# Attention scores as pairs of 64-row products, and softmax sums that are packed, inverted and spread by DMA

## Chip, cores and metric

One core of a Trainium2 chip runs the whole kernel in one launch. The metric is the device time of a run in microseconds; lower is better. The names of the engines are TensorE (PE, with its weight loads PEld), VectorE (DVE), ScalarE (ACT), GpSimd (POOL) and SyncE (SP), which only issues DMA transfers here.

## What is computed

The reference is two transformer-like layers on x of shape (2, 512, 512), all in float32: modulation, layer norm, attention, a routed low-rank expert block, then a second layer with weights in a 4-bit code. The change touches the attention of the first layer only:

```python
# 32 heads of size 16; 8 groups of keys and values, 4 heads to a group; S = 512
q = (x @ wq).reshape(b, s, 32, 16)
k = (x @ wk).reshape(b, s, 8, 16)      # each repeated for its 4 heads
v = (x @ wv).reshape(b, s, 8, 16)
scores = einsum('bihd,bjhd->bhij', q, k) * 16 ** -0.5
scores = where(causal, scores, finfo.min)
attn = softmax(scores, axis=-1)
out = einsum('bhij,bjhd->bihd', attn, v).reshape(b, s, 512)
return out @ wo
```

## The kernel before

Every engine has its program written out by hand; they meet at semaphores. The program runs through: modulation and layer norm with the projections of q, k and v (to 88 us of the trace), the attention stage (about 89 to 297 us), the output projection, the expert block, and the second layer, which takes two thirds of the time. While attention runs, the first 4-bit weights are decoded beside it in steps (`step_at`): ScalarE makes curves (L777), VectorE sums them (L1095), GpSimd scales them.

**Precision by parts.** A float32 value is kept as a rounded high part and a low part (FH and FL for the queries, KH and KL for the keys), and products are made of the parts.

**Stacks.** One stack holds one batch b and one group g: its number is n = 8 b + g, 16 in all, in three buffers. In `QS` (queries, stationary) rows 0 to 63 hold high, high, low, low parts of the group's 16 rows for 4 heads; in `KS` and `KN` (keys, moving) they hold high, low, high, low. The product over these 64 rows gives the exact score. Rows 64 to 127 of KS are zero; those of QS take a diagonal of the row maxima (L678, GpSimd), those of KN are -1. `load_stack` (L497, on SP) fills a stack by 12 transfers from SBUF to SBUF, four of 128 KB and eight of 32 KB. It waits until the stack three back is used up (`s_st`).

**Units.** A stack has four units, one for each block of 128 queries; unit n of 64 has (n % 4 + 1) * 128 keys, by causality. TensorE's order at step n is:
- `scores(n)` (L1532): for each of two halves, when the maxima of the same half of unit n - 1 are there, two heads of score products over 128 rows (L1540), each followed by a mask product of identB and maskB over 128 columns (L1542), then a signal. Four PSUM banks, one a head.
- `transposed(n - 2)` (L1546): the score products again with keys as output rows, now with KN, so that the maximum is subtracted (L1555, one per block of keys, three PSUM banks in turn, and a mask at L1558).
- on even n, `weighted(n - 4)` and `weighted(n - 3)` (L1563): exponentials times values, in four column tiles of 32, one a head (L1572, float32). V holds ones beside the values, so the sums of the softmax come out too, into bank 7.

VectorE at unit n takes the maxima of two heads twice (L1229), then the curve sum if one is due (slots 0, 1 and 7 of each eight units), then the work on a pair of groups: `copy_odd` in slot 2 (L1153, L1155) adds the odd group's bank 7 to NUM (values) and DEN (sums), of which ScalarE has copied the even group's (`copy_even`, L519); `swap_sums` in slot 3 shuffles the sums below the values they belong to (L1161); `invert` in slots 4 and 5 is a reciprocal of 256 columns each (L1165); `divide` in slot 6 (L1170). ScalarE takes the exponentials (L817) and rounds the divided heads (L797); VectorE splits them (L1177). The last pair's steps come after the loop.

## Time and profile before

| | |
|---|---|
| runs | 974.74, 969.53, 973.49 us; median 973.49 |
| profiled execution | 974.34 us, its span 972.50 us |
| mean granted TensorE clock | 0.97 of full speed |
| busy over the span | TensorE 891.2 us (92%), VectorE 707.7 (73%), ScalarE 528.5 (54%), GpSimd 190.3 (20%) |
| attention stage | 89 to 297 us |
| row maxima L1229 | 128 instructions, 99.6 us on VectorE |
| score products L1540 | 256 instructions |
| packets of DMA over the span | 91.6 MB, mean 94 GB/s |

Times are of one profiled execution, from the start of its span. Matmuls are pipelined: start plus duration of one is where it ends, and durations of neighbours overlap, so work on TensorE is best counted from end to end. A row of the timeline may hold several instructions of one kind (x24). "idle before <-releaser" tells how long the engine stood before an instruction and who ended that.

### The profile page before, as it was taken

The numbers are of one execution on the slowest core, as the hardware profiler recorded it, in microseconds if no ns is written. First come the engines' busy times: TensorE is split into PE (matmuls) and PEld (weight loads), VectorE is DVE, ScalarE is ACT, GpSimd is POOL, SyncE is SP. The second block draws the span as 40 slices with busy tenths as digits, with TensorE's granted clock in tenths as the row PEclk, the third lists the DMA queues.
The fourth block names the chain that finished last, engine by engine and source line by source line (L and its number), as shares of the span: only waits on it lengthen the run. The fifth ranks groups of instructions, "written<-read, shape, count | busy, mean of one in ns | idle before, by whom it ended". The sixth has DMA issues, their size and how long they took to land.

```text
span 972.5 us, 13806 instructions
## 1 busy us (share of the span) xinstructions
PE 891.2 (92%) x5240; PEld 684.8 (70%) x5240; DVE 707.7 (73%) x907; ACT 528.5 (54%) x695; POOL 190.3 (20%) x197
## 2 busy tenths in 40 slices
PE   3698899989889789897999999999969999999996
PEld 2456555556557568686888888688857888888885
DVE  4735789888879778788887776367887666766842
ACT  1512656656663424476766666366727666666830
POOL 3002456477557112300000000000040000000004
PEclk9798999999999989999999999889989999999999
DMA  9387466566534003105334323023312333332202
GB/s 325 104 270 150 57 102 108 73 106 109 67 71 158 11 13 101 29 22 155 109 99 113 107 88 95 14 86 98 108 34 62 106 93 87 109 97 71 71 1 87
DMA packets 40162, 91.61 MB, mean 94 GB/s; under 512 B 6944, under 2 KB 10144, under 8 KB 40096
## 3 DMA queue, kind: packets, MB, share of 16 engines
q1 hardware_dynamic: 35824, 85.23, 34.7%
q10 hardware_dynamic: 4272, 5.49, 1.6%
q8 instruction: 42, 0.69, 0.3%
q14 instruction: 24, 0.20, 0.1%
HBM read 76.02 MB, written 2.10 MB: 80 GB/s over the span
## 4 chain that ended last, share of the span: by engine, by line
PE 68%; DVE 5%; issue 3%; POOL 1%; ACT 1%; POOLq 0%; DVEq 0%; ACTq 0%
PE PS L1438 14%; PE PS L1439 14%; PE PS L1440 14%; PE PS L1749 5%; PE PS L1750 5%; PE PS L1748 5%; PE PS L1540 2%; PE PS L1572 1%; PE PS L1731 1%; POOL X L662 1%; PE PS L1555 1%; DVE MX L1229 1%; PE PS L1478 1%; PE PS L1490 1%; DVE SCR L1080 1%
## 5 line engine op out<-in xcount | busy, mean ns | idle before, releaser
L777 ACT ACTIVATE PL<-CODE 128x1024 f32<-128x1024 int32 x200 | 201.6, 1056 | 40.9 <-DVE ACC L1095 38.3
L1438 PE MATMUL PS<-HH,WRH 128*128 128x512 f32 x448 | 175.3, 391 | 0.0
L1439 PE MATMUL PS<-HH,WRL 128*128 128x512 f32 x448 | 175.1, 391 | 0.0
L1440 PE MATMUL PS<-HL,WRH 128*128 128x512 f32 x448 | 174.9, 390 | 0.0
L662 POOL TENSOR_TENSOR X<-X,SCR 128x512 f32<-128x512 f32 x32 | 42.1, 1326 | 574.3 <-DVE SCR L1080 574.2
L1095 DVE SCALAR_TENSOR_TENSOR ACC<-PL,ACC 128x1024 f32<-128x1024 f32 x100 | 124.5, 1245 | 8.4
L817 ACT ACTIVATE PT<-PS 128x512 f32<-128x512 f32 x160 | 85.2, 604 | 68.3 <-PE PS L1555 49.2
L1229 DVE TENSOR_REDUCE MX<-PS 128x2 f32<-128x256 f32 (+3 forms) x128 | 99.6, 818 | 20.2 <-PE PS L1542 12.7
L678 POOL TENSOR_TENSOR QS<-ident,MX 64x256 fp32r<-64x256 f32 x128 | 97.0, 758 | 68.1 <-DVE MX L1229 61.1
L1540 PE MATMUL PS<-KS,QS 128*128 128x128 f32 (+3 forms) x256 | 84.3, 411 | 15.8 <-DVE MX L1229 14.3
L1438 PEld LDWEIGHTS PS<-HH,WRH 128*128 128x128 f32 x448 | 84.6, 189 | 18.1 <-issue 0.8
L1440 PEld LDWEIGHTS PS<-HL,WRH 128*128 128x128 f32 x448 | 84.4, 188 | 17.5
L1439 PEld LDWEIGHTS PS<-HH,WRL 128*128 128x128 f32 x448 | 84.5, 189 | 17.0
L1385 DVE TENSOR_TENSOR HID<-SG,PS 128x512 f32<-128x512 f32 x56 | 38.2, 684 | 76.8 <-PE PS L1440 74.5
L1748 PE MATMUL PS<-WRH,HH 128*128 128x512 f32 x216 | 85.0, 394 | 0.0
L1750 PE MATMUL PS<-WRH,HL 128*128 128x512 f32 x216 | 84.9, 393 | 0.0
L1749 PE MATMUL PS<-WRL,HH 128*128 128x512 f32 x216 | 84.9, 393 | 0.0
L1540 PEld LDWEIGHTS PS<-KS,QS 128*128 128x128 f32 x256 | 51.3, 202 | 28.9 <-issue 14.0
L1095 DVE SCALAR_TENSOR_TENSOR ACC<-PL 128x1024 f32<-128x1024 f32 x50 | 62.1, 1242 | 12.0 <-ACT PL L777 11.7
L786 ACT ACTIVATE ACC<-ACC 128x1024 f32<-128x1024 f32 x50 | 53.1, 1061 | 32.1 <-DVE ACC L1095 32.1
L1555 PE MATMUL PS<-QS,KN 128*128 128x512 f32 x160 | 58.9, 449 | 7.3 <-ACT PT L817 7.0
L957 ACT ACTIVATE SG<-PS 128x512 f32<-128x512 f32 x56 | 32.8, 589 | 60.1 <-PE PS L1440 60.1
(226 smaller groups left out, 1565.7 us busy)
## 6 DMA issues: line engine op xcount, KB each, us to landing
CODE<-in_CODES SPq DMA_DIRECT2D x50, 512.0 KB, 3.5
SCALE<-in_SCALES SPq DMA_DIRECT2D x100, 256.0 KB, 4.0
WM<-in_WM SPq DMA_DIRECT2D x12, 1024.0 KB, 7.8
QS<-FH SPq DMA_DIRECT2D x32, 128.0 KB, 4.1
QS<-FL SPq DMA_DIRECT2D x32, 128.0 KB, 5.1
X<-in_X ACTq DMA_DIRECT2D x2, 1024.0 KB, 12.4
out_x<-X ACTq DMA_DIRECT2D x8, 256.0 KB, 2.0
WF<-in_LBGU SPq DMA_DIRECT2D x14, 128.0 KB, 3.8
```

What stands on the lines that cost most here:

```text
L678: nc.gpsimd.tensor_tensor(QS[64:P, q % STACKS, :, ic * P + 64 * half:ic * P + 64 * half + 64], ident[rows, rows].unsqueeze(1).to_broadcast ...
L777: nc.scalar.activation(PL[:, n % 3], CODE[:, p % 2], ACT.Prelu, scale=scale, bias=bias, alpha=alpha).then_inc(s_plane, 1)
L817: nc.scalar.activation(block_of(n, jc)[:].rearrange("p h i -> p (h i)"), PS[:, 4 + done % 3], ACT.Exp, scale=HD ** -0.5).then_inc(s_exp, 1)
L1095: nc.vector.scalar_tensor_tensor(acc, PL[:, at_plane % 3], CAPS[i], rest_of, ALU.min, ALU.add).then_inc(s_used, 1)
L1229: nc.vector.reduce_max(MX[:, n % 2, 2 * pair:2 * pair + 2], PS[:, 2 * pair:2 * pair + 2, 0:w], AX_X).then_inc(s_mx, 1)
L1438: nc.tensor.matmul(dst, lh, rh, start=start and k == 0, stop=False)
L1439: nc.tensor.matmul(dst, ll, rh, start=False, stop=False)
L1440: ins = nc.tensor.matmul(dst, lh, rl, start=False, stop=stop and k == KC - 1)
L1540: nc.tensor.matmul(PS[:, h, 0:(ic + 1) * P], QS[:, q % STACKS, h, ic * P:(ic + 1) * P], KS[:, q % STACKS, 0:(ic + 1) * P], start=True, sto ...
L1748: nc.tensor.matmul(dst[t], hh, wh, start=(n == 1 and k == 0), stop=False, skip_group_check=True)
L1749: nc.tensor.matmul(dst[t], hh, wl, start=False, stop=False, skip_group_check=True)
L1750: ins = nc.tensor.matmul(dst[t], hl, wh, start=False, stop=last and n == 1, skip_group_check=True)
```

## The change

- Score products: heads 0 and 1 stay in rows 0 to 63 of QS. Heads 2 and 3 go to rows 64 to 127 of a second stack `QB` (`later_heads`; stack 0 takes free rows of QS), and KS holds the keys twice, in both halves of the rows. A half unit is now two products over 64 rows each, at tile positions (0, 0) and (64, 0), into two banks, then the two masks. The halves are heads 0 and 2, then 1 and 3, and MX is written in that order.
- `load_stack` has 10 transfers in place of 12. Rows are laid out so that one transfer writes 32 partitions: each of the group's 16 rows twice (queries), or high and low side by side (keys, from the joint tile KHL). Queries now come to 768 KB a stack (was 512), keys to 384 KB (was 256). The queries' parts live in a joint tile FQ. The load of stack 1 as a whole waits for the last projection; before, only its keys for KN did.
- Sums: for all pairs but the last, SP packs the sums of a pair from 8 rows into a tile RC of 128 x 32 (two transfers), VectorE takes one reciprocal of RC in slot 4 (`invert_packed`), SP stores it to DRAM (two transfers), waits, and reads it back spread over all partitions into DENS (one transfer). `spread_sums` stands in SP's queue behind the load of stack 2 * pair + 4. `divide` moves to slot 0 of the pair after next, and waits for the spread. The last pair keeps shuffle and reciprocals.
- DEN shrinks to two pairs' sums in turn, and ScalarE's `copy_even` waits until the sums two pairs back are packed.
- The curve sum of slot 7 moves to slot 4. Two memsets (rows 64 to 127 of QS and of KS) go.

```diff
-    slots = (0, 1, 7)
+    slots = (0, 1, 4)
...
             if n == 0:
-                sp.wait_ge(s_ones, 2)
+                sp.wait_ge(s_ones, 1)
             if g == 0:
                 sp.wait_ge(s_free, J["k", b] + 1)
+            if n == 1:
+                sp.wait_ge(s_mm, J["v", B - 1] + 1)
             if n >= STACKS:
                 sp.wait_ge(s_st, STC(n - STACKS + 1))
...
-            for r, src in enumerate((FH, FH, FL, FL)):
-                sp.dma_start(QS[HD * r:HD * r + HD, n % STACKS].bitcast(F32), src[rows, :, cols].bitcast(F32)
-                             ).then_inc(s_qks[n % STACKS], 16)
-            for i, dst in enumerate((KS[:, n % STACKS], KN[n % STACKS])):
-                if (n, i) == (1, 1):
-                    sp.wait_ge(s_mm, J["v", B - 1] + 1)
-                for r, src in enumerate((KH, KL, KH, KL)):
-                    sp.dma_start(dst[HD * r:HD * r + HD].bitcast(F32), src[rows, cols].bitcast(F32)
-                                 ).then_inc(s_qks[n % STACKS], 16)
+            keys = KHL[rows, :, cols].bitcast(F32)
+            done = s_qks[n % STACKS]
+            for i in range(2):
+                queries = FQ[rows, i, b].unsqueeze(1).to_broadcast([HD, 2, REP, S]).bitcast(F32)
+                half = slice(32 * i, 32 * i + 32)
+                sp.dma_start(QS[half, n % STACKS].bitcast(F32), queries).then_inc(done, 16)
+                sp.dma_start(KS[half, n % STACKS].bitcast(F32), keys).then_inc(done, 16)
+                half = slice(64 + 32 * i, 96 + 32 * i)
+                sp.dma_start(later_heads(n, half).bitcast(F32), queries[:, :, REP // 2:]).then_inc(done, 16)
+                sp.dma_start(KS[half, n % STACKS].bitcast(F32), keys).then_inc(done, 16)
+            for i in range(2):
+                sp.dma_start(KN[n % STACKS][32 * i:32 * i + 32].bitcast(F32), keys).then_inc(done, 16)
+
+        def later_heads(n, rows):
+
+            return QS[rows, STACKS - 1, 0:REP // 2] if n == 0 else QB[rows, n % STACKS]
+
+        def spread_sums(sp, pair):
+
+            sp.wait_ge(s_odd, 2 * pair + 2)
+            for u in range(2):
+                sp.dma_start(RC[64 * u:64 * u + 64], DEN[HD * u:P:2 * HD, pair % 2]).then_inc(s_dn, 16)
+            sp.wait_ge(s_ri, pair + 1)
+            for u in range(2):
+                sp.dma_start(INV[:, 1 - u], RC[64 * u:64 * u + 64]).then_inc(s_rs, 16)
+            sp.wait_ge(s_rs, 32 * (pair + 1))
+            sp.wait_ge(s_div, pair)
+            sp.dma_start(DENS[:], INV.rearrange("h u s -> (h u) s").unsqueeze(1).to_broadcast([GROUPS, HD, S])
+                         ).then_inc(s_rb, 16)
...
             for n in range(B * GROUPS):
                 load_stack(sp, n)
                 for p in PIECES_AT.get(n, ()):
-                    load_piece(sp, p)
+                    load_codes(sp, p)
+                if n in SPREAD_AT:
+                    spread_sums(sp, SPREAD_AT[n])
+                for p in PIECES_AT.get(n, ()):
+                    load_scales(sp, p)
...
+            def invert_packed(pair):
+                dve.wait_ge(s_dn, 32 * (pair + 1))
+                nc.vector.reciprocal(RC[:], RC[:]).then_inc(s_ri, 1)
+
             def divide(pair):
                 b, c = divmod(pair, PAIRS)
+                if pair < B * PAIRS - 1:
+                    dve.wait_ge(s_rb, 16 * (pair + 1))
...
-                    nc.vector.reduce_max(MX[:, n % 2, 2 * pair:2 * pair + 2], PS[:, 2 * pair:2 * pair + 2, 0:w], AX_X
+                    nc.vector.reduce_max(MX[:, n % 2, pair::2], PS[:, 2 * pair:2 * pair + 2, 0:w], AX_X
                                          ).then_inc(s_mx, 1)
+                if pair_at(n, 2) is not None:
+                    copy_odd(pair_at(n, 2))
+                if pair_at(n, 4) is not None:
+                    invert_packed(pair_at(n, 4))
                 if step_at(n) and step_at(n)[1] < STEPS - 1:
                     curve_sum(*step_at(n))
                 if n == TB - 1:
                     gate_values()
-                if pair_at(n, 2) is not None:
-                    copy_odd(pair_at(n, 2))
-                if pair_at(n, 3) is not None:
-                    swap_sums(pair_at(n, 3))
-                for half in range(2):
-                    if pair_at(n, 4 + half) is not None:
-                        invert(half)
-                if pair_at(n, 6) is not None:
-                    divide(pair_at(n, 6))
+                if n >= 16 and n % 8 == 0:
+                    divide(n // 8 - 2)
+                if n == B * GROUPS * TB - 1:
+                    divide(B * PAIRS - 2)
...
                 for half in range(2):
                     if n >= 1:
                         pe.wait_ge(s_mx, 2 * (n - 1) + half + 1)
+                    cols = slice(ic * P, (ic + 1) * P)
+                    nc.tensor.matmul(PS[:, 2 * half, 0:(ic + 1) * P], QS[0:64, q % STACKS, half, cols],
+                                     KS[0:64, q % STACKS, 0:(ic + 1) * P], start=True, stop=True, tile_position=(0, 0))
+                    nc.tensor.matmul(PS[:, 2 * half + 1, 0:(ic + 1) * P], later_heads(q, slice(64, P))[:, half, cols],
+                                     KS[64:P, q % STACKS, 0:(ic + 1) * P], start=True, stop=True, tile_position=(64, 0))
                     for h in (2 * half, 2 * half + 1):
-                        nc.tensor.matmul(PS[:, h, 0:(ic + 1) * P], QS[:, q % STACKS, h, ic * P:(ic + 1) * P],
-                                         KS[:, q % STACKS, 0:(ic + 1) * P], start=True, stop=True)
                         ins = nc.tensor.matmul(PS[:, h, ic * P:(ic + 1) * P], identB[:], maskB[:], start=False, stop=True,
                                                skip_group_check=True)
```

## Rows read from the trace of the kernel before

**Rows 1.** A stretch of one pair: start:end and length, engines' busy time, clock, DMA

```profile
148.00:172.70 24.70, 22.46 (x255) 14.68 (x254) 22.21 (x27) 16.29 (x27) 15.34 (x18) 1.00 0.63 108
```

**Rows 2.** Who waits for whom on PE, 88 to 288 us: total, times, longest

```profile
PE PS L1540 <- DVE MX L1229: 14.3, 25, 1.6
```

**Rows 3.** Timeline of PE: score products of 512, then of 128 columns

```profile
171.18 0.50 PE L1540 MATMUL PS<-KS,QS 128*128 128x512 f32 x1
171.53 0.23 PE L1542 MATMUL PS<-maskB,identB 128*128 128x128 bf16 x1
171.57 0.47 PE L1540 MATMUL PS<-KS,QS 128*128 128x512 f32 x1
...
174.14 0.30 PE L1540 MATMUL PS<-KS,QS 128*128 128x128 f32 x1 [0.56 <-DVE MX L1229]
174.27 0.23 PE L1542 MATMUL PS<-maskB,identB 128*128 128x128 bf16 x1
174.31 0.31 PE L1540 MATMUL PS<-KS,QS 128*128 128x128 f32 x1
...
175.18 0.33 PE L1540 MATMUL PS<-KS,QS 128*128 128x128 f32 x1 [0.48 <-DVE MX L1229]
```

**Rows 4.** Timeline of PE where the shape of the tile changes

```profile
163.69 0.39 PE L1558 MATMUL PS<-identB,maskB 128*128 128x512 bf16 x1
164.01 0.86 PE L1572 MATMUL PS<-PT,V 128*32 128x128 f32 x24
164.81 0.38 PE L1540 MATMUL PS<-KS,QS 128*128 128x256 f32 x1
165.03 0.23 PE L1542 MATMUL PS<-maskB,identB 128*128 128x128 bf16 x1
165.07 0.36 PE L1540 MATMUL PS<-KS,QS 128*128 128x256 f32 x1
...
169.20 0.39 PE L1558 MATMUL PS<-identB,maskB 128*128 128x512 bf16 x1
169.52 1.74 PE L1572 MATMUL PS<-PT,V 128*32 128x128 f32 x56
...
294.75 1.98 PE L1490 MATMUL PS<-MR,sel 2*128 2x512 f32 x4
296.66 0.50 PE L1438 MATMUL PS<-WOH,FH 128*128 128x512 f32 x1
296.99 0.39 PE L1439 MATMUL PS<-WOH,FL 128*128 128x512 f32 x1
```

**Rows 5.** SP's issues of one stack, time to landing of KN's transfers, DMA beside them

```profile
168.01 1.34 SPq L510 DMA_DIRECT2D QS<-FH  x2
...
174.46 0.59 SPq L516 DMA_DIRECT2D KS<-KH  x1
...
KN<-KH SPq DMA_DIRECT2D x32, 32.0 KB, 2.0
...
169.00:172.00 3.00, 3.00 (x64) 2.12 (x63) 2.01 (x4) 0.60 (x1) 1.62 (x3) 1.00 1.03 197
172.00:175.00 3.00, 2.14 (x13) 1.16 (x11) 2.97 (x4) 1.09 (x2) 0.00 (x0) 1.00 0.94 108
```

**Rows 6.** Timeline of DVE in slots 2 to 4, and all reciprocals of the stage

```profile
171.32 0.75 DVE L1153 SCALAR_TENSOR_TENSOR NUM<-PS,HALVES,NUM 128x512 f32<-128x512 f32 x1 [0.99 <-PE PS L1572]
172.77 2.36 DVE L1229 TENSOR_REDUCE MX<-PS 128x2 f32<-128x1024 f32 x2
175.05 0.74 DVE L1161 STREAM_SHUFFLE DENS<-DEN 128x512 f32<-128x512 f32 x1
175.82 0.76 DVE L1229 TENSOR_REDUCE MX<-PS 128x2 f32<-128x256 f32 x2
176.50 1.74 DVE L1165 RECIPROCAL DENS<-DENS 128x256 f32<-128x256 f32 x1
...
L1165 DVE RECIPROCAL DENS<-DENS 128x256 f32<-128x256 f32 x14 | 24.4, 1743 | 0.0
```

49 lines of the change are left out of this document (30 added, 19 removed).

## The prediction

> **What bounds the kernel now.** The profiled execution took 974.34 us, 1.84 us more than its span of 972.50 and 0.85 us more than the median of the runs (973.49). Everything the change touches lies in the attention stage, 89 to 297 us: 64 units (16 stacks of a batch and a group, four query blocks each). I read the stage by the table of stretches first. A stretch of eight units (two stacks, one pair; the numbers 0 to 7 below are their slots) lasts 24.70 us, with TensorE busy 22.5 and VectorE 22.2 at the full clock [rows 1]. Both look like the bound, so the second view is who waits for whom on TensorE: in 200 us it waited 14.3 us for row maxima [rows 2]. It has work for about nine tenths of the stage; a longer or shorter TensorE program shows in the time.
>
> The third view, TensorE's timeline, says where VectorE holds it up. In every pair the largest such place is the step from a full-width unit to the first unit of the next stack: the first 128-wide score product starts after 0.56 us of waiting, the second half after 0.48 [rows 3]. VectorE's timeline shows why: it is idle 0.99 us until the weighted values are done, adds the odd group (L1153, L1155), and only then takes the maxima of the full-width unit, 2.36 us [rows 6]. It is not late from earlier work; it is a chain. Shuffle, reciprocals and division come after it, and beside them TensorE shows no wait for maxima until the next full-width unit. VectorE is nearly full there, but in time.
>
> **Part 1, score products.** One head costs TensorE, from end to end (start plus duration), the step from the mask's end to the next product's end, plus the mask. Steps: 0.28 us at 512 columns (171.76 to 172.04), 0.12 at 128 (174.50 to 174.62) [rows 3], 0.17 at 256 (165.26 to 165.43) [rows 4], so 0.23 at 384. The mask adds 0.07. Two heads (a half unit) cost 0.70, 0.60, 0.48 and 0.38 us.
>
> After the change a half unit is one pair of 64-row products side by side and two masks at 128 rows. That the two overlap I take from the column tiles of L1572: 8 groups of four take 0.88 us more (1.67 against 0.79 from the mask's end), 0.11 a group [rows 4], less than the 0.12 of one single 128-column step [rows 3]. So the second tile adds about 0.01. The price is the change of tile shape. Into 32-column tiles: 0.79 us less 6 groups of 0.11 leaves 0.13. Out of them: the 256-wide product ends 0.32 after the last one, in place of 0.17, so 0.15. Out of a 2-row product (L1490, the only row shape there is before): 0.43 to the end of L1438 against 0.22 for the next, so 0.21 [rows 4]. No row shows 64 rows; the bounds are 0 (no charge between these two shapes) and 0.21, and I take 0.15, which both directions of the nearest row give. Every half unit has two such changes, 256 in all.
>
> A half unit then costs step + 0.15 + 0.01 + 0.07 + 0.15 + 0.07, that is 0.73, 0.68, 0.62 and 0.57 us: +0.03, +0.08, +0.14, +0.19 for 512 down to 128 columns, +0.44 over a stack for one half, times 32 = +14 us of TensorE work. Not all shows. In the first unit of a stack TensorE waits for the second half's maxima anyway [rows 3], so the first half's extra 0.19 is covered (16 times, 3 us), and a shape change that falls into such a wait costs nothing (0.15 x 16 = 2.4 us). I take +8 us; with 0.13 a change it is +3 us, with 0.21 +20 us.
>
> The Trainium skill, TensorEngine Tiling (Array Packing), Key Properties, says that changing the tiling mode, not just the tile, drains TensorE. It gives no figure; the trace agrees for the shapes it has. The same page's Theoretical Speedup (up to 2x for 64 rows), taken without the drain, is the first rival below.
>
> **Part 2, sums packed and inverted.** Off VectorE per pair: one shuffle (0.74) and two reciprocals of 1.74 (14 in the loop, 24.4 us) [rows 6]. On it: one reciprocal of 32 columns, by width 1/8 of 1.74, about 0.25 us. That is 4.0 us a pair, 28 us over seven pairs, and I cost it at nothing: none of it stands ahead of the maxima that TensorE waits for. If it did, the most to win is the wait for maxima outside the chain, a few of the 14.3 us [rows 2]. The last pair keeps its old form, and its tail stays. Copies, division and splits keep size; the memsets taken from GpSimd stood ahead of the whole stage. The curve sum moved from every eighth unit's slot 7 to slot 4 fills time that the reciprocals leave.
>
> **Part 3, SP's queue.** Now a stack is 12 transfers, 768 KB. SP needs 6.45 us to issue the first six, because the DMA engines are full (share 1.03 and 0.94, 197 then 108 GB/s), and 0.63 for each later one [rows 5]. After: 10 transfers, 4 x 0.63 us less at best, but 1152 KB in all (768 KB queries, 384 KB keys), each twice as many partitions. Bounds for issuing: 6.3 us (ten at 0.63) and, at the present rate of 576 KB in 6.45 us, 1024 / 89 + 1.3 = 12.8 us. The rate is not fixed (197 with two destinations in flight), and twice the partitions should be nearer to it; I take 7 us. Once per pair five transfers join: two packings, a wait for VectorE, two stores, a wait for them, and the spreading. With 2.0 us to land as for KN [rows 5] the way is 2.6 + 0.3 + 2.7 + 0.6 = 6.2 us, in which SP issues nothing else; the next stack's load stands behind it. A load is released six units (18 us) before its stack starts, so 6.2 + 7 + 2 = 15 us still fits.
>
> VectorE's new wait is the packed reciprocal in slot 4. SP's load was released at 168.01 and VectorE is through with slot 4's maxima at 176.58, 8.6 us later [rows 5, 6]. 7 + 0.6 + 2.0 = 9.6 us: VectorE stands 1.0 us. Behind it are queued the curve sum and the next maxima, for which TensorE waits. The reciprocal that is gone (1.5 us) covers it, less the curve sum (1.2) in two of three pairs. I charge +1 us over six pairs, since TensorE has other work for part of it. The division waits for the spread inverses in slot 0, four units later, 12 us against about 7: hidden. The second stack's load now waits for the last projection, and its ten issues fit beside the first stack's four units: hidden too.
>
> Sum: 974.3 + 8 + 1 = 983.3 for the profiled execution, 982.5 as a median.
>
> **Rivals.** (1) No charge for going between 128 and 64 rows. A half unit costs step + 0.15: 0.43, 0.38, 0.32, 0.27, so -0.27, -0.22, -0.16, -0.11, times 32 = -24 us. Of it the chain keeps the full-width unit after the odd group (0.54 x 8 = 4.3), half of the other (2.2) and the first half of a stack (1.8): -16 us, with SP's +1 a time of 958.5. VectorE's relief is what allows it. For: no row shows a 64-row tile. Against: every change of shape in the trace costs 0.13 us or more, the 2-row one too. By the Trainium skill, TensorE: Matmul & The Clock Gate, Measured speedup vs the span model, packed tiles add about 4 ns each and no change of mode is charged; that is this rival's rule.
>
> (2) SP is late (slower). If a load takes more than 8 us to issue, the packed sums land over 2 us after VectorE asks, and the rest falls on the maxima; over 9.7 us, two loads and the spreading (2 x 9.7 + 6.2) are longer than a pair, and SP sets the pace. At 9.5 us it costs 1.5 x 6 = 9 us (992), at the full 12.8 us 31.8 - 25.5 = 6.3 us a pair, 38 us (1020); centre 1000. For: share 1.03 already, half as many bytes again. Against: the rate of 197 GB/s.
>
> (3) The two tiles run one after the other, so the change doesn't do what it says: the second product's step (mean 0.20) comes back 128 times, +26 us on the forecast: 1008.
>
> **Chances.** Forecast 0.50, with 976 to 992 as its own range; (1) 0.22; a shape change of about half the price, which ends near no change, 0.10; (2) 0.13; (3) 0.05. The measurement can tell about 0.5% from no change, 968.6 to 978.4. Faster: (1) and a little of the halfway case, 0.25. Same: the rest of it and the forecast's low edge, 0.17. Slower 0.58. The range 957 to 1000 takes in half of (1) and the near part of (2).
>
> **What the profile after should show.** Part 1: in TensorE's timeline the two products of a half unit start within 0.02 us, and the first mask ends 0.2 us or more after them; if it ends 0.07 after, rival 1 has it, and if the second product ends a whole step after the first, rival 3. A pair takes 25.5 to 26 us against 24.7. Part 2: VectorE's busy time falls by some 4 us a pair while the pair doesn't get shorter; if the wait for maxima falls much below 14 us, my reading of the chain was wrong. Part 3: ten issues of a load in 6.3 to 8 us, and little idle time of VectorE before the packed reciprocal; 3 us or more there means rival 2. The prediction fails most likely on the price of the shape change between 128 and 64 rows, the one term that no row shows.

## The result, and the profile after

The changed kernel takes 1018.81 us (median of four runs, 1016.85 to 1019.98), the kernel before beside it 973.9 us. The ratio is 1.047, 95% interval 1.043 to 1.050: slower by 45 us. The forecast was 982.5, the range ended at 1000. The profiled execution has a span of 1016.7 us against 972.5, and the last unit's first maxima start at 327.6 us against 286.0: 41.6 of the 44.2 us are in the attention stage.

A stretch of one pair after, to be read beside [rows 1] (same columns: start:end, length, busy PE, PEld, DVE, ACT, POOL, clock, DMA share, GB/s):

```profile
144.50:177.40 32.90, 26.12 (x252) 15.06 (x252) 17.79 (x24) 15.60 (x27) 13.51 (x18) 0.84 0.82 122
```

The pair takes 32.9 us instead of 24.7. Neither engine that filled it before is full now, VectorE least of all, and TensorE's clock is down to 0.84. That points to something that is no compute engine. Who waits for whom, whole execution (total, times, longest), and the chain of waits:

```profile
DVE RC L1206 <- DMA RC<-DEN: 41.5, 6, 8.0
...
PE 72%; SPq 11%; DVE 6%; issue 4%; DMA 3%; ACT 2%; POOL 1%; POOLq 0%; DVEq 0%; ACTq 0%
```

and of the kernel after in 88 to 288 us, the row that answers to [rows 2]:

```profile
PE PS L1586 <- DVE MX L1272: 30.6, 23, 4.4
```

VectorE stands 41.5 us before the packed reciprocal, about as much as the stage grew (whether the one makes the other is for the experiments), and SyncE's queue, with nothing in the chain before, holds 11% of it. SyncE's and VectorE's timelines of the same pair (start, duration, engine, line, out<-in, count, idle before):

```profile
151.82 0.62 SPq L528 DMA_DIRECT2D QS<-FQ  x1
...
161.17 2.02 SPq L534 DMA_DIRECT2D KN<-KHL  x2
163.23 1.22 SPq L544 DMA_DIRECT2D RC<-DEN  x2
166.38 1.12 SPq L547 DMA_DIRECT2D inverses<-RC  x2
168.74 0.62 SPq L550 DMA_DIRECT2D DENS<-inverses  x1
169.40 0.65 SPq L528 DMA_DIRECT2D QS<-FQ  x1
...
180.42 0.68 SPq L478 DMA_DIRECT2D CODE<-in_CODES  x1
...
182.72 0.62 SPq L528 DMA_DIRECT2D QS<-FQ  x1
```

```profile
157.63 0.42 DVE L1272 TENSOR_REDUCE MX<-PS 128x2 f32<-128x256 f32 x1 [0.30 <-PE PS L1591]
166.00 0.35 DVE L1206 RECIPROCAL RC<-RC 128x32 f32<-128x32 f32 x1 [7.95 <-DMA RC<-DEN]
```

The load of a stack takes 11.4 us to issue (151.82 to 163.23), then come 6.2 us of packing, storing and spreading, a load of 11.0 and the weight pieces of 2.3: 30.9 us from one load to the same place in the next pair, with no time between. The sums are in DEN when VectorE has done its copies (154.6), but their packing stands behind the load. VectorE asks at 158.05 and gets them at 166.00.

The slots tell the same with all pairs in it. Labels are those of the experiments below. The numbers are the mean time from the first maxima of one unit to those of the next (VectorE's timeline, the six pairs in the middle); the last column is their sum.

| kernel | 0 | 1 | 2 | 3 | 4 | 5 | 6 | 7 | pair |
|---|---|---|---|---|---|---|---|---|---|
| before | 2.34 | 2.86 | 4.26 | 3.27 | 2.45 | 3.00 | 3.48 | 3.23 | 24.9 |
| after | 3.47 | 2.93 | 4.23 | 2.37 | 9.25 | 1.64 | 5.28 | 2.64 | 31.8 |
| scores_alone | 2.31 | 2.90 | 4.25 | 3.22 | 3.01 | 3.37 | 3.92 | 3.45 | 26.4 |
| scores_wide | 2.22 | 2.89 | 4.25 | 3.22 | 2.65 | 3.00 | 3.28 | 3.45 | 25.0 |
| curve_moved | 3.34 | 3.00 | 4.23 | 3.15 | 3.75 | 3.08 | 3.69 | 2.59 | 26.8 |
| wide_pack_first | 3.51 | 2.88 | 4.52 | 2.37 | 3.79 | 3.20 | 4.01 | 2.64 | 26.9 |
| wide_slots | 2.22 | 2.92 | 4.25 | 2.39 | 3.33 | 2.80 | 3.39 | 3.45 | 24.8 |
| sums_pack_first | 5.01 | 2.43 | 5.09 | 2.37 | 3.98 | 3.08 | 3.95 | 2.63 | 28.5 |
| pack_first | 4.29 | 2.71 | 4.66 | 3.64 | 4.70 | 3.34 | 3.76 | 3.22 | 30.3 |
| pack_slots | 3.49 | 3.55 | 4.53 | 3.92 | 4.01 | 2.86 | 3.42 | 3.98 | 29.8 |

TensorE's timeline after, the products that answer to [rows 3] (512, then 128 columns):

```profile
153.05 0.49 PE L1586 MATMUL PS<-KS,QS 64*128 64x512 f32 x1
153.06 0.50 PE L1588 MATMUL PS<-KS,QB 64*128 64x512 f32 x1
153.49 0.29 PE L1591 MATMUL PS<-maskB,identB 128*128 128x128 bf16 x2
...
154.14 0.29 PE L1591 MATMUL PS<-maskB,identB 128*128 128x128 bf16 x2
...
156.01 0.29 PE L1586 MATMUL PS<-KS,QS 64*128 64x128 f32 x1 [0.83 <-DVE MX L1272]
156.01 0.33 PE L1588 MATMUL PS<-KS,QB 64*128 64x128 f32 x1
```

The two tiles of a half unit start within 0.01 us of each other and the second adds nothing. From the end of one pair of masks (153.49 + 0.29 = 153.78) to the end of the next (154.43) a half unit costs 0.65 us. The two products overlap as intended; what the score part costs comes below.

### The profile page after: what moved, and what is told of

Same layout as the page of the kernel before. It is cut to its first block, busy times and chain, and to the rows that moved or that the text cites. A ratio compares the mean times of both kernels' runs of the same rounds, so it can differ in the third digit from the quotient of the medians.

```text
span 1016.7 us, 13795 instructions
## 1 busy us (share of the span) xinstructions
PE 912.1 (90%) x5240; PEld 680.4 (67%) x5240; DVE 683.4 (67%) x886; ACT 529.7 (52%) x695; POOL 180.8 (18%) x195
## 4 chain that ended last, share of the span: by engine, by line
PE 72%; SPq 11%; DVE 6%; issue 4%; DMA 3%; ACT 2%; POOL 1%; POOLq 0%; DVEq 0%; ACTq 0%
PE PS L1480 15%; PE PS L1481 15%; PE PS L1482 15%; PE PS L1799 5%; PE PS L1797 5%; PE PS L1798 5%; SPq L531 4%; PE PS L1621 2%; SPq L529 2%; SPq L534 2%; SPq L528 2%; DMA RC<-DEN 2%; PE PS L1586 1%; SPq L532 1%; DMA WM<-in_WM 1%
## 5 line engine op out<-in xcount | busy, mean ns | idle before, releaser
L716 POOL TENSOR_TENSOR QS<-ident,MX 64x256 fp32r<-64x256 f32 x128 | 93.0, 726 | 108.3 <-DVE MX L1272 101.5
L1586 PE MATMUL PS<-KS,QS 64*128 64x128 f32 (+3 forms) x128 | 57.5, 449 | 38.3 <-DVE MX L1272 34.6
L1604 PE MATMUL PS<-QS,KN 128*128 128x512 f32 x160 | 64.7, 488 | 9.2 <-ACT PT L855 7.6
L1586 PEld LDWEIGHTS PS<-KS,QS 64*128 64x128 f32 x128 | 25.8, 202 | 64.2 <-DVE MX L1272 34.9
```

What stands on the lines that cost most here:

```text
L716: nc.gpsimd.tensor_tensor(QS[64:P, q % STACKS, :, ic * P + 64 * half:ic * P + 64 * half + 64], ident[rows, rows].unsqueeze(1).to_broadcast ...
L1586: nc.tensor.matmul(PS[:, 2 * half, 0:(ic + 1) * P], QS[0:64, q % STACKS, half, cols], KS[0:64, q % STACKS, 0:(ic + 1) * P], start=True, st ...
```

## The experiments

Each is named by its label. "Kernel before" and "after" are the two of this case; ratios are to the kernel before, run beside it on the same chip. In a diff, ... stands for lines left out.

### Each part alone

**scores_alone**: the row-group products and the new loads, sums as before (shuffle, two reciprocals, division in slot 6, curve sum in slot 7).

```diff
-    slots = (0, 1, 4)
+    slots = (0, 1, 7)
...
-                if n in SPREAD_AT:
-                    spread_sums(sp, SPREAD_AT[n])
...
-                    invert_packed(pair_at(n, 4))
+                    swap_sums(pair_at(n, 3))
```

> The score products in pairs of 64 rows with the new loads of the stacks, the sums as before (shuffle and two reciprocals on VectorE, nothing of them on SP). In the changed kernel SP is never idle in a pair: a load takes 11.4 us, two of them and the 6.2 us of spreading set the pace. Theory 'queue': without the spreading two loads (22.8 us, and 2.3 us of 4-bit weights in some pairs) just fit into a pair of 24.7 us, and TensorE's half units cost the same as before within 0.1 us (0.64 against 0.71 us at 512 columns, 0.47 against 0.38 at 128), so 973 to 980 us. Theory 'tiles' (my forecast: the changes of tile shape cost TensorE some 14 us): 982 us or more, with the extra in TensorE's own steps.

Measured 981.57 us, ratio 1.0076 (1.005 to 1.010): above the range of 'queue', at the edge of 'tiles'. **sums_alone**: the other part alone, spread sums with the curve sum in slot 4 and the loads and products of before.

> Only the packed, inverted and spread sums; score products and the loads of the stacks as before. Theory 'queue': a load keeps its 10.2 us of issuing, so two loads and the spreading are 26.6 us in a pair of 24.7, and the packed sums reach VectorE 10.2 + 0.6 + 2.0 - 8.6 = 4.2 us late in each of six pairs: 985 to 995 us. If the relief of VectorE (4 us a pair) were worth something by itself: below 974 us.

Measured 1007.04 us, ratio 1.034 (1.031 to 1.037). The loss is above all with the sums, and they cost 12 us more than the top of what I expected. VectorE waited 28.0 us at the packed reciprocal, in six places (41.5 after). SyncE's queue is full in scores_alone too: a load runs from 145.89 to 157.24, and the next starts at once. Under scores_wide it turns out that its 8 us don't come from there.

```profile
145.89 0.62 SPq L528 DMA_DIRECT2D QS<-FQ  x1
...
155.24 1.99 SPq L534 DMA_DIRECT2D KN<-KHL  x2
157.27 0.69 SPq L528 DMA_DIRECT2D QS<-FQ  x1
```

**no_inverts**: the kernel before without the shuffle and the reciprocals of all pairs but the first (that part of the computation is left out).

```diff
-                if pair_at(n, 3) is not None:
+                if pair_at(n, 3) == 0:
                     swap_sums(pair_at(n, 3))
...
-                    if pair_at(n, 4 + half) is not None:
+                    if pair_at(n, 4 + half) == 0:
                         invert(half)
```

> The kernel before without the shuffle and the two reciprocals in every pair but the first (the division uses the first pair's inverses, so that part of the computation is left out). It gives VectorE back 4.2 us a pair and adds nothing anywhere. My reading of the chain (TensorE never waits for what stands behind the maxima): within 3 us of before, 971 to 974. Theory 'VectorE is the bound': 2 us a pair or more, 960 us or less.

Measured 969.81 us, ratio 0.9963 (0.995 to 0.998), 1 us below what I expected. The whole relief that the spread sums can give to VectorE is worth 4 us, if it costs nothing at all. TensorE's wait for maxima, 14.3 us in [rows 2], stays near that:

```profile
PE PS L1540 <- DVE MX L1229: 13.1, 23, 1.6
```

### The score products

**masks_behind**: the kernel before, with the two masks of a half unit behind its two products, 128 rows as they were.

```diff
                     for h in (2 * half, 2 * half + 1):
                         nc.tensor.matmul(PS[:, h, 0:(ic + 1) * P], QS[:, q % STACKS, h, ic * P:(ic + 1) * P],
                                          KS[:, q % STACKS, 0:(ic + 1) * P], start=True, stop=True)
+                    for h in (2 * half, 2 * half + 1):
                         ins = nc.tensor.matmul(
```

> The kernel before, with the two mask products of a half unit issued behind its two score products, not one behind each. In the changed kernel's trace the second of two masks in a row costs 0.055 us, not 0.07, and in the kernel before one full-shape product right behind another of its kind costs 0.227 us at 512 columns, against 0.284 behind a mask. So a half unit should cost 0.07 us less, 128 times: 9 us less TensorE work, 963 to 968 us if TensorE bounds the stage, 971 or more if the waits for maxima take it back.

Measured 968.63 us, ratio 0.9949 (0.993 to 0.997), the only version that computes everything and is faster than both kernels; it lies just above the 963 to 968 us that I expected. **tiles_in_turn**: the same, with 64-row products one after the other in the same row group.

```diff
-                        nc.tensor.matmul(PS[:, h, 0:(ic + 1) * P], QS[:, q % STACKS, h, ic * P:(ic + 1) * P],
-                                         KS[:, q % STACKS, 0:(ic + 1) * P], start=True, stop=True)
+                        nc.tensor.matmul(PS[:, h, 0:(ic + 1) * P], QS[0:64, q % STACKS, h, ic * P:(ic + 1) * P],
+                                         KS[0:64, q % STACKS, 0:(ic + 1) * P], start=True, stop=True,
+                                         tile_position=(0, 0))
```

> The kernel before with score products over its 64 rows of data only (row group 0, tile position (0, 0)), two in a row and then the two masks: the changes of shape of the changed kernel, but no two tiles side by side, and no other load or queue. By the steps seen in the changed kernel (0.42 us into the 64-row shape at 512 columns, 0.16 for the first mask, 0.055 for the second) and 0.23 for the second product, a half unit costs 0.86 us at 512 columns and 0.53 at 128, 0.15 us more than before: +19 us of TensorE work, some 4 us of it covered, 985 to 990 us. If changes of shape cost what I had forecast (0.30 us a pair of changes, not 0.23): 995 us or more. If they cost nothing here: 970 us.

Measured 989.32 us, ratio 1.016 (1.010 to 1.023), as expected. TensorE at 512 columns, first masks_behind, then tiles_in_turn:

```profile
168.39 0.28 PE L1543 MATMUL PS<-maskB,identB 128*128 128x128 bf16 x2
168.49 0.72 PE L1540 MATMUL PS<-KS,QS 128*128 128x512 f32 x2
169.05 0.28 PE L1543 MATMUL PS<-maskB,identB 128*128 128x128 bf16 x2
```

```profile
152.84 0.29 PE L1544 MATMUL PS<-maskB,identB 128*128 128x128 bf16 x2
153.06 0.73 PE L1540 MATMUL PS<-KS,QS 64*128 64x512 f32 x2
153.72 0.29 PE L1544 MATMUL PS<-maskB,identB 128*128 128x128 bf16 x2
```

A half unit from masks to masks is 0.66 us with 128 rows, 0.88 with 64 rows in turn, 0.65 with 64 rows side by side (above). So the change of tile shape costs 0.22 us a half unit, in and out together, and the overlap of the two tiles gives back 0.23. At this width the gain from row groups is real and its price is of the same size. At the smaller widths the price is larger than the gain. In the same measure (median ends, full clock) masks_behind takes 0.66, 0.53, 0.42 and 0.36 us for 512 down to 128 columns, the kernel after 0.65, 0.59, 0.53 and 0.48: over 128 half units 9 us more TensorE work than the same masks behind products over 128 rows.

### The loads

**wide_sources**: the kernel after, with each load's transfers reading rows once, from twice as many rows (a group has 16; where an expectation gives 32 and 64 rows it is 16 and 32). Bytes and number of transfers are the same, the data in the stacks are another group's too, so scores are not the reference's.

```diff
-            keys = KHL[rows, :, cols].bitcast(F32)
+            wide = slice(HD * (g - g % 2), HD * (g - g % 2) + 2 * HD)
+            keys = KHL[wide, 0, cols].bitcast(F32)
...
-                queries = FQ[rows, i, b].unsqueeze(1).to_broadcast([HD, 2, REP, S]).bitcast(F32)
+                queries = FQ[wide, i, b].bitcast(F32)
```

> The changed kernel, but each transfer of a stack reads 32 partitions of the source once instead of 16 twice, same bytes, same destinations (so queries and keys are of the wrong rows). Theory 'source': the loads run at 105 GB/s because every read of a stack comes from the same 16 partitions; then a load takes 6.5 to 7.5 us, VectorE hardly waits for the packed sums, and the time is 972 to 982 us. Theory 'bytes': the rate is that of the engines or of the destination; then the load stays at 11.4 us and the time at 1019 us.

Measured 993.92 us, ratio 1.020 (1.016 to 1.024): 25 us back, not all. The load is as short as 'source' has it, the time lies between the two theories. Its SyncE, and its row of waits at the packed reciprocal:

```profile
148.48 0.54 SPq L529 DMA_DIRECT2D QS<-FQ  x1
...
155.46 1.24 SPq L545 DMA_DIRECT2D RC<-DEN  x2
```

```profile
DVE RC L1207 <- DMA RC<-DEN: 7.3, 5, 2.2
```

**scores_wide**: scores_alone with the same edit.

> The run with the new scores and loads alone (981.6 us), but each load's transfers read 64 rows once where they read 32 rows twice: the same bytes and the same number of transfers, other data in the stacks, so the scores are not the reference's. If the 7.5 us by which the new scores and loads are slower than the kernel before come from the longer loads (11.2 us where before's take 7), this gives 970 to 976 us, the loads issue in 7 us, and the clock goes back to that of before. If they come from the row tiles (entries and exits), it stays at 979 us or more.

Ratio 1.008 (1.004 to 1.012), median 980.1 us. Loads take 6.9 us (154.15 to 161.07 in its timeline; a load of the kernel before takes 10.2, not the 7 of the expectation). The ratio is that of scores_alone: by the medians the shorter loads gave nothing back, and by the expectation's own measure that speaks against the loads as the cause. Ten runs went from 970.7 to 986.8 us, with the mean granted clock going from 0.964 down to 0.943, and the profiled one (span 968.8 us) is the fastest of them. In it the slots are those of the kernel before within 0.3 us each (25.0 us a pair against 24.9). scores_alone has 1.4 us a pair more, in slots 4 to 6. It doesn't wait for stacks there: in these six pairs TensorE never waits for a load. Two rows of scores_alone, a pair at full clock and a stretch of slots 4 to 6, and the kernel before in the second stretch:

```profile
140.20:165.00 24.80, 22.35 (x255) 12.89 (x253) 21.44 (x26) 15.22 (x27) 14.98 (x20) 1.00 0.95 140
178.00:188.00 10.00, 10.00 (x83) 5.75 (x77) 6.81 (x7) 3.54 (x7) 3.78 (x6) 0.50 0.84 87
```

```profile
178.00:188.00 10.00, 9.24 (x98) 6.14 (x98) 8.53 (x11) 6.19 (x11) 3.46 (x7) 1.00 0.60 68
```

With loads of 11 us and the DMA share at 0.95 a pair of scores_alone takes 24.8 us when TensorE's clock is granted in full. Pairs take 26.7 us and more where the clock falls to 0.50 in slots 4 to 6, as it does in four of the six and never there in the kernel before. What stands ahead of the fall is the step in [rows 3]: TensorE is through with the full-width unit sooner and waits longer for VectorE,

```profile
175.23 0.30 PE L1580 MATMUL PS<-KS,QS 64*128 64x128 f32 x1 [0.83 <-DVE MX L1265]
```

0.83 us and then 0.49, where the kernel before waits 0.56 and 0.48. But the two pairs at full clock have the same waits (0.83 and 0.50), so what makes the clock fall in one pair and not in the next isn't shown. In this execution, which lies at the median of the runs (981.74 us), what the score part loses comes with the lower clock, not with a wait for the loads.

Why a load takes 7.0 or 11.4 us, read in stretches in which nothing but stack loads moves: first two of the kernel before, then one of after, then one of scores_wide (length, busy times, clock, DMA share, GB/s):

```profile
159.00:162.00 3.00, 2.98 (x19) 1.67 (x15) 1.94 (x3) 2.83 (x4) 1.09 (x2) 1.00 0.95 102
184.00:186.00 2.00, 2.00 (x11) 1.04 (x10) 1.26 (x2) 1.37 (x3) 0.76 (x2) 1.00 0.98 103
```

```profile
158.00:161.00 3.00, 3.00 (x30) 1.59 (x28) 0.05 (x1) 2.19 (x4) 1.99 (x3) 0.50 0.99 104
```

```profile
157.00:160.00 3.00, 2.94 (x35) 1.50 (x23) 2.26 (x3) 2.45 (x4) 1.54 (x2) 1.00 0.84 184
```

With 16 source rows the transfers carry 102 to 104 GB/s, whether they write 16 rows (before) or 32 (after); with 32 source rows 184. The source's rows set the rate. 1152 KB at 104 GB/s are 11.3 us, the load's length. (At 32 source rows the DMA engines have room, share 0.84, so 184 GB/s need not be their limit.) The Trainium skill, SBUF — State Buffer, section Door 1: The DMA port swizzle, gives 104 GB/s for a transfer of 1 MiB on partitions 0 to 15 and 189 for 0 to 31; the trace agrees for sources inside SBUF, with 102 to 104 and 184.

### The wait at the packed reciprocal

**invert_later**: the kernel after with that wait in slot 7.

```diff
-                if pair_at(n, 4) is not None:
-                    invert_packed(pair_at(n, 4))
+                if pair_at(n, 7) is not None:
+                    invert_packed(pair_at(n, 7))
```

> The changed kernel with the packed reciprocal three units later in VectorE's order (slot 7, not 4). Theory 'queue' (SP is full: two loads, the spreading and the 4-bit weights are as long as the pair): VectorE's wait for the packed sums goes, but the pair stays at 29 us or more, 1005 to 1020 us. Theory 'late wait' (SP keeps up, only VectorE asks too early): the 41 us that it waits come back, 980 us.

Measured 1027.79 us, ratio 1.056 (1.050 to 1.063), slower still and 8 us above the range of 'queue'. Now SyncE waits: its queue, and its row of waits.

```profile
169.11 1.43 SPq L544 DMA_DIRECT2D RC<-DEN  x2
178.22 1.13 SPq L547 DMA_DIRECT2D inverses<-RC  x2
```

```profile
SPq L547 <- DVE RC L1206: 43.4, 7, 12.0
```

The store waits for the reciprocal with the next load behind it. So with the wait taken from VectorE, SyncE has it, and what stands behind it in SyncE's queue is late.

**sums_by_act** and **after_by_act**: sums_alone and after with the five transfers issued by ScalarE, behind the exponentials of slots 2, 4 and 5, and the packed reciprocal in slot 5.

```diff
+                if n >= 8 and n % 8 == 2:
+                    pack_sums(act, n // 8 - 1)
+                if n >= 8 and n % 8 == 4:
+                    store_inverses(act, n // 8 - 1)
+                if n >= 8 and n % 8 == 5:
+                    spread_inverses(act, n // 8 - 1)
                 ride(n + 3)
```

> The kernel before with the sums packed, inverted and spread by transfers, as in the run with the sums alone (1007.0 us), but the five transfers of a pair are issued by ScalarE, behind the exponentials of the third, fifth and sixth unit, so that no wait of theirs stands on SyncE; the packed reciprocal is one slot later. If SyncE's queue made those 33 us, the pair goes back to about 25 us, SyncE keeps two loads and the pieces in it, the loads issue in 6.3 to 7 us, and the time is 968 to 978 us (ScalarE gives up 5 issues of 0.6 us a pair, 3 us of some 9 that it has idle). If the transfers' own landing times or VectorE's wait at the packed reciprocal made it, wherever they are issued, it stays at 995 us or more.

> The changed kernel (1018.8 us) with the five transfers of the sums issued by ScalarE in the same places. If SyncE's queue with both parts on it (two loads of 11 us, pieces of 2 us, spreading of 6 us) is the cause, SyncE keeps 24.6 us of it, as in the run with the new scores and loads alone (981.6 us), and the time is 976 to 990 us. If the transfer engines are short of rate for all of it, or the waits for the sums make it, it stays at 1005 us or more.

Measured 997.62 us (ratio 1.028, 1.024 to 1.032) and 1038.79 us (1.074, 1.067 to 1.081). Both lie in the second case of their expectations, in which SyncE's queue is not the cause. But ScalarE's timeline of sums_by_act, where that queue had room, shows where the wait went:

```profile
161.37 1.41 ACTq L535 DMA_DIRECT2D inverses<-RC  x1
...
165.23 0.62 ACTq L541 DMA_DIRECT2D DENS<-inverses  x1
165.90 1.06 ACT L804 ACTIVATE PL<-CODE 128x1024 f32<-128x1024 int32 x1 [1.93 <-DMA inverses<-RC]
```

ScalarE stood for the stores to land, with curves and exponentials behind. In after_by_act such waits on ScalarE come to 21.4 us in five places, and VectorE waited 18.5 us for the spread inverses. The runs say nothing for or against SyncE's queue as the cause: they took the waits from it and gave them to an engine that is busy itself, and both still hold the moved curve sum (below). **masks_sums_act**, masks_behind with the sums of sums_by_act, came to 1001.59 us, ratio 1.032 (1.026 to 1.037), the second case of its expectation; nothing is gained.

> The kernel before with the masks of a half unit behind its two score products (alone 968.6 us) and the sums spread by transfers that ScalarE issues. VectorE is relieved of the shuffle and the inversion (worth 4 us where they were left out) and ScalarE gets 3 us a pair. Expected 963 to 970 us; if the issues and waits on ScalarE hold up exponentials that the next product waits for, 972 us or more.

### Order in the queue, and the length of it

**pack_first** (on after), **wide_pack_first** (on wide_sources), **sums_pack_first** (on sums_alone): only the two packing transfers move, ahead of the load.

```diff
             for n in range(B * GROUPS):
+                if n in SPREAD_AT:
+                    pack_sums(sp, SPREAD_AT[n])
                 load_stack(sp, n)
```

> The changed kernel (1018.8 us), with the two transfers that pack the sums issued by SyncE ahead of the stack's load instead of behind it. Nothing else moves. If the loss is VectorE's wait at the packed reciprocal (41.5 us in six pairs) and that alone, it goes, and the time is 976 to 985 us. If SyncE's queue sets the pace as well, the pair stays as long as what is issued in it: two loads of 11.4 and 11.0, pieces of 2.1, packing 1.2, stores with their landing 2.4, the spreading 0.6, that is 28.7 us and up to 1.5 more for the wait for the copies, against 31.5 in the changed kernel; 2 us a pair less, 1000 to 1008 us.

> Both suspected causes away: the loads read each source row once, from twice as many rows (7.0 us to issue; other data in the stacks, so the scores are not the reference's; 993.9 us so far), and the packing is issued ahead of the load. SyncE then has about 23 us of work in a pair of 24.7. If the queue is the whole cause, this ends at 968 to 978 us, where the new scores and loads alone in this form are. If the sums cost something else (the division in slot 0, the moved curve sum, the clock), it stays at 985 us or more.

> The kernel before with the spread sums alone (1007.0 us), the packing issued ahead of the load. Loads take 10.2 us here, so SyncE has 10.2 + 10.2 + 1.75 + 1.2 + 2.4 + 0.6 = 26.4 us and the wait for the copies, against 24.7. If the order in the queue is the cause, the 28 us of waiting at the packed reciprocal go and the time is 978 to 990 us; if it is not, it stays above 1000 us.

Measured 1011.14 us (ratio 1.040, 1.037 to 1.043), 990.83 (1.018, 1.015 to 1.021) and 998.82 (1.028, 1.023 to 1.033). The first is 3 us above the case in which the queue's length counts too, the second says that something besides the queue costs, the third lies between its cases. The waits at the packed reciprocal fall from 41.5 to 4.8 us, from 7.3 to nothing and from 28.0 to 2.5, but the time of the changed kernel only by 8 us. In pack_first TensorE now waits for the stacks themselves:

```profile
153.74 1.24 SPq L544 DMA_DIRECT2D RC<-DEN  x2
...
184.61 0.62 SPq L544 DMA_DIRECT2D RC<-DEN  x1
```

```profile
PE PS L1592 <- DMA KN<-KHL: 17.1, 8, 4.8
```

184.61 less 153.74 is 30.9 us, the same round as in the kernel after. The place in the queue decided where the stall shows, the length of the queue how long it is. But wide_pack_first has a queue with room (SyncE waits 46.7 us for the copies there) and still loses 18 us, and sums_pack_first 26 us. Slots 0 and 4 grow most in both (and slot 2 in sums_pack_first), and those two kernels share two more edits: the moved curve sum and the division in slot 0.

### The curve sum

**curve_moved**: the kernel before with one number changed.

```diff
-    slots = (0, 1, 7)
+    slots = (0, 1, 4)
```

> The kernel before with one number changed: the curve sum of slot 7 in slot 4, as the change has it. Everything else, shuffle and reciprocals included, is as before. If the move by itself costs, by the fold and the scaling that follow it and stand ahead of a diagonal on GpSimd, this takes 978 to 992 us. If it is free, as the prediction had it, 970 to 976 us.

Measured 982.92 us, ratio 1.012 (1.008 to 1.017), the first case of the expectation: 11 us for an edit that I had costed at nothing. ScalarE's, GpSimd's and TensorE's timelines:

```profile
150.52 1.06 ACT L786 ACTIVATE ACC<-ACC 128x1024 f32<-128x1024 f32 x1
...
151.71 1.58 POOL L634 TENSOR_TENSOR WT<-ACC,SCALE 128x512 f32<-128x512 f32 x1 [5.50 <-DVE MX L1229]
153.37 1.30 POOL L678 TENSOR_TENSOR QS<-ident,MX 64x256 fp32r<-64x256 f32 x2
...
154.81 0.94 PE L1555 MATMUL PS<-QS,KN 128*128 128x512 f32 x3 [1.71 <-POOL QS L678]
...
160.33 2.73 PE L1572 MATMUL PS<-PT,V 128*32 128x128 f32 x56
```

The move shifts the steps of the decoding on ScalarE as well. The fold (L786) ends at 151.58, only then can GpSimd scale (L634, though the releaser is given as VectorE's), and the diagonal of slot 4 stands behind the scaling in GpSimd's order. TensorE waits 1.71 us for it, and in what follows the granted clock is 0.50, the lower level (1.2 GHz):

```profile
157.00:162.00 5.00, 5.00 (x43) 3.15 (x45) 3.26 (x4) 1.20 (x2) 3.00 (x5) 0.50 0.64 68
```

The 56 column-tile products take 2.73 us here, 1.74 in [rows 4]. Over all pairs slots 0 and 4 grow by 1.0 and 1.3 us, slot 7 gives back 0.6. The division stands in slot 6 here as before, so slot 0 grows without it; with it, in wide_pack_first, slot 0 has 0.2 us more.

**wide_slots** (on wide_pack_first), **sums_slots** (on sums_pack_first), **pack_slots** (on pack_first): the curve sum back in slot 7, the division in slot 4 instead of slot 0. These runs move both, and only curve_moved has one of them alone.

```diff
-    slots = (0, 1, 4)
+    slots = (0, 1, 7)
...
-                if n >= 16 and n % 8 == 0:
+                if n >= 16 and n % 8 == 4:
                     divide(n // 8 - 2)
```

> The run with both queue causes away (990.8 us, loads of 7 us and the packing ahead of the load; other data in the stacks, so the scores are not the reference's), and in it the curve sum back in slot 7, as in the kernel before, and the division in slot 4 instead of slot 0. If the 20 us that remain come from what stands in slots 0 and 4 on VectorE (curve sum and division one behind the other in slot 0; curve sum, fold, scaling and diagonals in one row of waits in slots 4 and 5), the slots 0 (3.5 us), 4 (3.8) and 6 (4.0) go back to 2.3, 2.7 and 3.3, and the time is 966 to 976 us. If they come from the transfers or the clock alone, it stays at 985 us or more.

> The kernel before with the spread sums and the packing issued first (998.8 us), the curve sum back in slot 7 and the division in slot 4. If the slots cost what they seem to in the kernels with short loads, 15 us and more come back: 976 to 985 us, the rest being SyncE's queue (26.4 us and a wait in a pair of 24.7). If only the queue counts, it stays at 995 to 1000 us.

> The changed kernel with the packing ahead of the load (1011.1 us), the curve sum back in slot 7 and the division in slot 4. The loads keep their 11.4 us. If the placing on VectorE costs what it costs in the other kernels (11 us alone in the kernel before, 12 and 13 us in the two others) whatever the queue does, this takes 996 to 1001 us. If SyncE's queue sets the pace of a pair by its length (some 29 to 31 us of issues and landings), the placing is hidden behind it and it stays at 1006 to 1012 us.

Measured: wide_slots 978.78 us, ratio 1.005 (1.002 to 1.008), 3 us above the first case of its expectation; sums_slots 986.02 us, ratio 1.014 (1.009 to 1.018), 1 us above; pack_slots 1006.05 us, ratio 1.035 (1.032 to 1.038). In the profiled execution of wide_slots (span 968.5 us) a pair of the changed kernel, with short loads, the packing first and the curve sum in its old place, is as long as one of the kernel before (24.8 and 24.9 us; what slot 4 gets, slot 3 gives). But that execution is the fastest of ten (970.4 to 980.6 us, clock 0.965 down to 0.950), so that nothing is left of the loss holds for this execution and not for the others. The median keeps 0.5%, 7 us, about as much as scores_alone and scores_wide lose, and like them this kernel has the 64-row products and a lower clock than the kernel before (0.965 to 0.971). The rest of the loss is the length of the queue, the order in it and the placing. In pack_slots the third is worth 5 us, where it was 12 to 13 in the two others, as if the queue's length (29.8 us a pair) hides it; the time lies above the 996 to 1001 us of an addition and at the edge of the case in which the queue alone sets the pace.

## Why the prediction was wrong, and where it was right

**The direction was right, the mechanism that I chose was not.** I forecast a small loss on TensorE and 1 us on SyncE's queue. The loss is the other way round. Rival 2, with a chance of 0.13, is what happened: SyncE is late and sets the pace. That its 38 us for a load of 12.8 us come near the 41.6 us by which the stage grew is luck. At the 11.4 us that the loads took its formula gives 2 x 11.4 + 6.2 - 25.5 = 3.5 us a pair, 21 us; it left out the weight pieces (2.3 us in the pair shown), and the curve sum has a part in the rest.

**Part 1, the price of the tiles: the term was mis-sized.** The charge for going into 64-row tiles is 0.14 us, as forecast (0.15). Coming out, the first mask ends 0.16 us after the tile, so 0.09 for the charge and not 0.15, and the second mask adds 0.055, not 0.07. A half unit after costs 0.65, 0.59, 0.53 and 0.48 us for 512 down to 128 columns (median ends in TensorE's timeline), where I had 0.73, 0.68, 0.62 and 0.57. Measured in the same way the kernel before has 0.71, 0.60, 0.49 and 0.38. The sum over 128 half units is some +2 us of work, not +14. That the score part by itself loses 8 us (scores_alone), as I had forecast, is luck: the forecast's +8 was for charges, and these 8 are the lower clock in slots 4 to 6. I had taken my price from changes between a 32-column tile and the full array and applied it to every neighbour, the two masks included. The tiles overlap fully, so rival 3 is out; rival 1, no charge at all, is out by tiles_in_turn, which pays 0.22 us a half unit. Rival 3 reckoned 34 us over the kernel before for tiles in turn (8 of the forecast, 26 of second products); tiles_in_turn lost 15. The charges in it were too high as in mine, and a second product right behind another costs 0.23 us at 512 columns and 0.11 at 128, not the mean of 0.20 that it took from products behind a mask.

**Part 2, the relief of VectorE: right.** Costed at nothing, worth 4 us at most (no_inverts). The reading of the chain in [rows 3] and [rows 6] holds: without shuffle and reciprocals TensorE's wait for maxima is 13.1 us, against 14.3. But one edit in the same paragraph was waved through: the curve sum's move "fills time that the reciprocals leave". On VectorE it does. It also moves a curve, a fold and a scaling on two other engines, and the scaling stands ahead of a diagonal that TensorE waits for. By itself it costs 11 us (curve_moved). The steps of a moved operation have to be followed to every engine that they touch; I followed one.

**Part 3, SyncE's queue: the step that failed.** The 7 us for issuing a load, and with it the claim that two loads and the spreading fit into a pair. I bounded a load's issue by 6.3 and 12.8 us and took 7, because of the 197 GB/s in the first of the two stretches of [rows 5]. That stretch isn't stack loads alone. The kernel before had just issued a transfer of the weights' codes (512 KB) and two of their scales (256 KB each) from DRAM, and the load that starts at 168.01 isn't over at 174.46 either:

```profile
166.27 1.15 SPq L475 DMA_DIRECT2D SCALE<-in_SCALES  x2
168.01 1.34 SPq L510 DMA_DIRECT2D QS<-FH  x2
...
177.62 0.60 SPq L516 DMA_DIRECT2D KN<-KL  x1
```

The second stretch, 108 GB/s, was the rate of the loads, and 102 and 103 in two others of the same trace. Half as many bytes again at that rate is 11 us, and most of the loss could have been reckoned blind from it: 11.4 + 11.0 + 6.2 + 2.3 = 30.9 us against 24.9 is 36 us over six pairs. The argument that twice the destination rows would raise the rate is refuted by after itself (104 GB/s with 32 rows written). The prediction's own rows already gave a load of the kernel before as 6.45 + 6 x 0.63 = 10.2 us, so 7 us for half as many bytes again asked for a shorter load than the one that was there. It was not set against the pair either: two loads and the pieces filled 22.2 of SyncE's 24.7 us before the change (10.2 + 10.2 + 1.8), and nothing on the page of the profile counts that as busy.

**The wait and its cover.** Given 11.4 us for the load, the step's own formula gives 11.4 + 0.6 + 2.0 less 8.6, that is 5.4 us of VectorE standing, where six waits come to 41.5 us, 6.9 each. In the wait shown, 7.95 us, the load began at 151.82, 6.2 us before VectorE asked at 158.05 and not 8.6: it had no time to start earlier, since SyncE had issued without a break up to it. That a load is released 18 us before its stack starts, "so 6.2 + 7 + 2 = 15 us still fits", fails with it: it looks at one load, and two loads, the pieces and the spreading are 30.9 us a pair. The cover that I counted (0.3 to 1.5 us of VectorE's time a pair) is small against either. The division's wait for the spread inverses was hidden, as I had said: the kernel after has none.

**Signs set in advance.** A pair of 25.5 to 26 us: 31.8. A load issued in 6.3 to 8 us: 11.4. The two products start within 0.02 us: seen. First mask 0.2 us or more behind the tiles: 0.16, between the two cases. Wait for maxima much below 14 us would have been wrong: it rose to 30.6 (this tests little, since VectorE is late itself; no_inverts is the clean test). Idle time of 3 us or more before the packed reciprocal means rival 2: 7.95 us.

**What stays open.** The parts add up to less than the whole: 8 us for the scores' part alone, 33 for the sums' alone, 45 together. Three causes make the loss but for some 7 us, and queue and placing hide each other in part. Curve sum and division were not moved back one at a time. How much of the loss is TensorE's lower clock was not taken apart: in 88 to 288 us it is 0.97 before, 0.91 in scores_alone and 0.87 after. Why the clock falls more with the 64-row products, and why ten runs of scores_wide differ by 16 us with it, isn't known. No run has masks_behind's products with the new loads, which would tell the tiles' share from that of the DMA traffic.

## What to carry to other kernels

Count the queue that only issues transfers as an engine: add up, over one period, the issues, the landings that it waits for and the time in which it is held up by full DMA engines, and compare that with the period before anything is put into it. Take a transfer's rate from a stretch in which only such transfers run, and ask first how many rows the source spans. When a step is moved, follow its helpers to each engine's order; the cheap edit in the middle of a large change (one number in a tuple) costs by itself as much as a quarter of the loss. When a median and a profile disagree, ask which of the runs was profiled, and read the granted clock slot by slot before a wait is blamed. The best version found is the smallest: two masks behind two products, 0.5% faster than the kernel before.

## What the runs showed of the hardware

- A transfer inside SBUF from 16 source rows ran at 102 to 104 GB/s with the DMA engines' share at 0.95 to 0.99; from 32 source rows, same bytes, at 184 GB/s. The number of rows written (16 or 32) made no difference. A share near 1 therefore didn't mean that the engines were at their best rate.
- Two 64-row products in different row groups start within 0.01 us and cost together what one costs. Going from 128 rows into them cost 0.14 us and coming back 0.09, and after that a second mask added 0.055. With the masks behind both products a half unit of 512 columns took 0.66 us with 128 rows, against 0.71, and at 128 columns 0.36, where the 64-row pair took 0.48.
- A store to DRAM of 16 KB in two transfers, from issue to the release of the transfer behind it, took 2.4 us (166.38 to 168.74), the way from the packing's issue to the reciprocal's end 3.1 us.
- TensorE's granted clock fell after idle time of its own, though not after all of it. In curve_moved it idled 1.7 us at 153.1 and the clock was 0.50 from 157 to 162 us. In the kernel after it idled from 163.7 to 168.1, and then:

```profile
168.00:171.00 3.00, 2.92 (x14) 1.32 (x17) 2.49 (x4) 0.00 (x0) 1.22 (x2) 0.50 0.29 72
```

So a wait can cost more than its own length: the work behind these ran at the lower of the two levels, 1.2 GHz, for some microseconds. After the 0.56 and 0.48 us of [rows 3] the clock stayed at 1.00; after 0.83 and 0.49 us in scores_alone it stayed at 1.00 in two pairs and fell to 0.50 in four.
